# Attention scores of a graph network: source products made with folded query weights, biases by a row of ones

## What is computed

```python
q = x @ wq + bq
k = x @ wk + bk
v = x @ wv + bv
e = edge_attr @ we
ke = k[src] + e
score = jnp.sum(q[dst] * ke, axis=-1) / jnp.sqrt(jnp.asarray(ke.shape[-1], x.dtype))
smax = jax.ops.segment_max(score, dst, num_segments=n_nodes)
a = jnp.exp(score - smax[dst])
denom = jax.ops.segment_sum(a, dst, num_segments=n_nodes)
alpha = a / denom[dst]
msg = alpha[:, None] * (v[src] + e)
out = jax.ops.segment_sum(msg, dst, num_segments=n_nodes)
out = out + x @ ws + bs
```

## Time and profile before

| | us |
|---|---|
| median of 3 runs | 7116.05 (7091.61 to 7118.32) |
| profiled execution | 7111.88 |
| its span in the trace | 7110.1 |
| TensorE, VectorE, ScalarE, GpSimd busy | 4507.4, 4533.2, 1627.7, 4000.1 |
| last dense output of at1s, start | 3794.1 |
| last dense output of at2s, start | 5066.4 |

### The profile page before, as it was taken

How to read it: one execution, slowest core, us unless ns; L and a number is a source line. 1 busy time by engine, 2 the same in 40 slices (tenths; PEclk the granted TensorE clock), 3 DMA queues, 4 the chain that set the end, 5 groups by cost and what they waited for, 6 DMA issues and landing times. The chain is left out here.

```text
span 7110.1 us, 101720 instructions
## 1 busy us (share of the span) xinstructions
PE 4507.4 (63%) x31722; PEld 4047.3 (57%) x31722; DVE 4533.2 (64%) x5921; ACT 1627.7 (23%) x2291; POOL 4000.1 (56%) x3348
## 2 busy tenths in 40 slices
PE   4666335771067878266665846777587765784797
PEld 2355234661057778266665846666587764673675
DVE  6999544220567778399998833333687974782458
ACT  0044112330033344133332421111144430000001
POOL 0099466556067768777762877775000007757766
PEclk9866667995589999678887978999899987997999
DMA  6498666664932257333333844444377872222109
GB/s 245 151 275 266 157 145 139 139 138 66 360 101 72 74 174 257 88 98 98 98 94 114 263 144 123 132 135 128 103 243 267 311 283 62 53 57 88 14 12 289
DMA packets 850501, 1076.78 MB, mean 151 GB/s; under 512 B 589151, under 2 KB 601844, under 8 KB 848956
## 3 DMA queue, kind: packets, MB, share of 16 engines
q1 hardware_dynamic: 547292, 794.01, 34.7%
q0 software_dynamic: 144256, 90.12, 8.9%
q10 hardware_dynamic: 158560, 187.31, 7.9%
HBM read 608.19 MB, written 469.22 MB: 152 GB/s over the span
## 5 line engine op out<-in xcount | busy, mean ns | idle before, releaser
L857 POOL DMA_INDIRECT gc_msgs<-t,src_rows x784 | 756.3, 965 | 1142.6 <-POOLq L147 847.1
L911 POOL DMA_INDIRECT acc<-de_sums,de_put x392 | 609.2, 1554 | 416.3 <-DMA acc<-de_sums,de_put 268.9
L1953 PEld LDWEIGHTS gc_ring<-gc_msgs,gc_hot 128*128 128x128 f32 x4736 | 621.1, 208 | 313.3 <-issue 305.2
L1953 PE MATMUL gc_ring<-gc_msgs,gc_hot 128*128 x4736 | 647.5, 295 | 238.1 <-SPq L1912 236.9
L857 POOL DMA_INDIRECT edge_rows<-h,dst_rows x392 | 478.0, 1219 | 242.2 <-DMA h<-at1w_win 126.0
L857 POOL DMA_INDIRECT edge_rows<-x,dst_rows x392 | 505.5, 1290 | 167.7 <-issue 117.1
L1045 PE MATMUL de_ring<-de_win,de_pick 128*128 x2368 | 343.9, 306 | 267.1 <-DMA de_win<-t 267.1
L1045 PEld LDWEIGHTS de_ring<-de_win,de_pick 128*128 128x128 f32 x2368 | 323.4, 218 | 289.3 <-issue 284.4
L857 POOL DMA_INDIRECT at1s_ends<-x,src_rows x392 | 398.0, 1015 | 150.5 <-issue 121.1
L857 POOL DMA_INDIRECT re_rows<-x,src_rows x392 | 408.7, 1043 | 125.3 <-issue 125.0
L857 POOL DMA_INDIRECT at2s_ends<-h,src_rows x392 | 372.9, 951 | 174.4 <-issue 116.5
(11 more groups left out here) (479 smaller groups left out, 11362.9 us busy)
## 6 DMA issues: line engine op xcount, KB each, us to landing
rew_win<-x SPq DMA_DIRECT2D x74, 544.0 KB
at1w_win<-g SPq DMA_DIRECT2D x74, 544.0 KB
at2w_win<-g SPq DMA_DIRECT2D x74, 544.0 KB, 4.1
de_near<-same SPq DMA_DIRECT2D x74, 512.0 KB, 5.2
de_win<-t SPq DMA_DIRECT2D x74, 512.0 KB, 4.5
x<-rew_win SPq DMA_DIRECT2D x74, 512.0 KB
h<-at1w_win SPq DMA_DIRECT2D x74, 512.0 KB
h<-at2w_win SPq DMA_DIRECT2D x74, 512.0 KB, 2.9
```

The source lines that it names most:

```text
L857: nc.gpsimd.indirect_dma_start(buf[:, t * width:(t + 1) * width], None, table, bass.IndirectOffsetOnAxis(ap=rows[:, t:t + 1], axis=0)).the ...
L911: nc.gpsimd.indirect_dma_start(g.acc0[j % 2], bass.IndirectOffsetOnAxis(ap=put[:, j:j + 1], axis=0), sums[:, j * D:(j + 1) * D], None, com ...
L1953: done = nc.tensor.matmul(ring[:, bass.ds(to[n], SLOT)], hot[k][:, n, :], each_group(msgs[:, bass.ds(of[n], MID)], SLOT // MID), start=Fal ...
```

## The change

Scores are computed as relu(x_dst) . u, where u holds, for every edge, the query weights times (k + e): the weights wk·wqᵀ and [we; bk]·wqᵀ are made once per stage, on TensorE, by `lay_out` on VectorE and ten lines ahead of TensorE's batches. The query bias becomes one more column for each tile of a pair, so a product is 258 columns wide: 128 of u, 128 of v, 2 of bias terms. Four of these fill four banks, psU. Attributes are transposed into 64 rows (4 transposes in place of 2), and a 65th row of ones brings the biases of k and v. Destination rows are no longer scaled, transposed, copied with relu or multiplied: `dot` reads them where they lie, relu and product in one instruction, and the sum is scaled afterwards (8 columns) in at1s. ScalarE's new step `keep` copies v to the destination rows' place and the bias terms into `scores`; `score` then adds the two. The dense products of at2s come 256 columns wide, both weights side by side. ScalarE's order is written out.

The last pair comes four times. The transposes of destination rows and the query products are gone, 14 transposes ahead of the pieces are 12, and 16 products are 8 wide ones. The core of the diff:

```diff
                 def turn(b):
                     ...
-                    for k in range(B // 2):
-                        nc.tensor.transpose(psD[:, k * P:(k + 1) * P], values[:, b.number * W + k * P:b.number * W + (k + 1) * P], g.ident[:, :])
-                    transpose_pairs(nc, psE, ea[s % 2], g.ident, B // 4)
+                        nc.tensor.transpose(psE[0:D, k * P:(k + 1) * P], ea[s % 2][:, k * D:(k + 1) * D], g.ident[:, :])
                 def project(b):
                     ...
-                    times(nc, psQ, hdT[s % 2], wq, B // 2)
-                    for to, w in ((psK, wk), (psV, wv)):
-                        for h in range(2):
-                            nc.tensor.matmul(to[:, h * 256:(h + 1) * 256], eaT[s % 2][:, h * P:(h + 1) * P], we[:, :], start=True, stop=False,
-                                             skip_group_check=True)
...
+                    for j in range(B // 2):
+                        nc.tensor.matmul(psU[:, j, 0:PUT], eaT[s % 2][0:D + 1, j * P:(j + 1) * P], from_attr[:, :], start=True, stop=False,
+                                         skip_group_check=True)
+                        last = nc.tensor.matmul(psU[:, j, 0:PUT], hsT[s % 2][:, j * P:(j + 1) * P], from_src[:, :], start=False, stop=True,
+                                                skip_group_check=True)
 # own
-                            times(nc, psY, xT[s % 2][:, h * W:(h + 1) * W], g.w[dense[n][0]], B // 2).then_inc(piece, 1)
+                            times(nc, psY, xT[s % 2][:, m * EACH * P:(m + 1) * EACH * P], own_w, EACH).then_inc(piece, 1)
 # ScalarE
-                    nc.scalar.activation(hdT[s % 2][:, :], psD[:, :], ACT.Relu)
+                def keep(b):
+                    act.wait_ge(dotted, b.number + 1)
+                    nc.scalar.activation(grouped(far(b), P), psU[:, :, P:2 * P], ACT.Copy)
+                    nc.scalar.activation(grouped(scores[:, bass.ds(b.number * B, B)], 2), psU[:, :, 2 * P:PUT], ACT.Copy).then_inc(used, 1)
-                    pipeline(act, order=[(1, root), (1, turn), (0, square), (4, nothing)], slots=SLOTS)
+                    written_out(order=[(1, root), (2, keep), (1, turn), (0, square)], slots=SLOTS)
 # VectorE
-                    nc.vector.tensor_tensor(grouped(far(b), D), grouped(far(b), D), spread(root[:, 0, B:J], D), ALU.mult)
+                def dot(b):
+                    if not normalise:
+                        dve.wait_ge(ahead[b.slot], 16 * B * b.nth)
+                    dve.wait_ge(product, b.number + 1)
+                    nc.vector.scalar_tensor_tensor(grouped(dots[:, :], P), grouped(far(b), P), 0.0, psU[:, :, 0:P], ALU.max, ALU.mult).then_inc(dotted, 1)
+                    dve.wait_ge(dotted, b.number + 1)
+                    link(nc.vector.tensor_reduce(found[:, :], grouped(dots[:, :], D), AXX, ALU.add))
+                    if normalise:
+                        link(nc.vector.tensor_tensor(found[:, :], found[:, :], sd[b.slot % 2][:, 0, B:J], ALU.mult))
                 def score(b):
...
+                    at = scores[:, bass.ds(b.number * B, B)]
                     dve.wait_ge(used, b.number + 1)
+                    link(nc.vector.tensor_tensor(at, at, found[:, :], ALU.add))
                     link.restart()
...
+                    pipeline(dve, order=[(1, variance), (1, scale), (2, dot), (2, take(0)), (2, score), (0, centre), (2, take(1))], slots=SLOTS)
+                    pipeline(dve, order=[(2, dot), (2, take(0, 1)), (2, score), (2, take(2, 3))], slots=SLOTS)
```

More of the change, by code:

```diff
@@ L1455, in attention_scores @@
     bq, bk, bv = (g.w[n] for n in biases)
-    pieces = [(h, n) for n in range(len(dense)) for h in range(2)]
-    M = len(pieces)
+    N2 = len(dense)
+    EACH = 4 // N2
+    M = J // 2 // EACH
+    PUT = 2 * P + 2
     with Room(nc, g, name + "s") as r:
@@ L1461, in attention_scores @@
         ea = [r.sb(f"ea{k}", [P, B * DE]) for k in range(2)]
-        outs = [[r.sb(f"out{n}{k}", [P, C]) for k in range(2)] for n in range(len(dense))]
-        hsT, hdT, eaT, xT = ([r.sb(f"{n}{k}", [P, w]) for k in range(2)] for n, w in (("hsT", W), ("hdT", W), ("eaT", B * DE), ("xT", C)))
-        q, k_ = g.zeros[:, 0:W], g.zeros[:, W:2 * W]
+        outs = [r.sb(f"outs{k}", [P, N2 * C]) for k in range(2)]
+        hsT, eaT, xT = ([r.sb(f"{n}{k}", [P, w]) for k in range(2)] for n, w in (("hsT", W), ("eaT", W), ("xT", C)))
+        dots, found = g.zeros[:, 0:W], g.zeros[:, W:W + B]
+        from_src, from_attr = r.sb("from_src", [P, PUT]), r.sb("from_attr", [D + 1, PUT])
+        key_rows, query_bias = r.sb("key_rows", [D + 1, P]), r.sb("query_bias", [P, P])
+        own_w = g.w[dense[0][0]] if N2 == 1 else r.sb("own_w", [P, N2 * P])
+        own_b = r.sb("own_b", [P, N2, 2, D])
+        tipped_w = xT[0]
+        KEY, ATTR, QUERY, BIAS = 0, P, 2 * P, 3 * P
         if normalise:
@@ L1507, in inputs_ready @@
                 eng.wait_ge(got[b.slot], 16 * B * b.nth)
-                eng.wait_ge(ahead[b.slot], 16 * B * b.nth)
                 eng.wait_ge(ea_in[b.slot], 32 * b.nth)
@@ L1597, in _, with lay_out @@
                 link = Link(dve, link_s)
+                def lay_out():
+                    v = nc.vector
+                    v.tensor_copy(key_rows[0:D, :], we[0:D, 0:P])
+                    v.tensor_copy(grouped(key_rows[D:D + 1, :], D), each_group(bk[D:D + 1, :], 2))
+                    v.tensor_copy(grouped(query_bias[:, :], D), each_group(bq[:, :], 2)).then_inc(laid, 1)
+                    for k in range(2):
+                        v.memset(eaT[k][D:D + 1, :], 1.0)
+                    for n, (_, bias, _) in enumerate(dense):
+                        v.tensor_copy(own_b[:, n, :, :], each_group(g.w[bias][:, :], 2))
+                        if N2 > 1:
+                            v.tensor_copy(own_w[:, n * P:(n + 1) * P], g.w[dense[n][0]][:, :])
+                    v.tensor_copy(from_src[:, P:2 * P], wv[:, :])
+                    v.tensor_copy(from_attr[0:D, P:2 * P], we[0:D, 0:P])
+                    v.tensor_copy(grouped(from_attr[D:D + 1, P:2 * P], D), each_group(bv[D:D + 1, :], 2))
+                    link(v.memset(tipped_w[:, BIAS:BIAS + 2], 0.0))
+                    dve.wait_ge(tipped, 1)
+                    v.tensor_copy(tipped_w[:, 0:ATTR + D + 1], psS[:, 0:ATTR + D + 1])
+                    v.tensor_copy(tipped_w[:, QUERY:QUERY + P], psS[:, QUERY:QUERY + P])
+                    v.tensor_copy(tipped_w[0:D, BIAS:BIAS + 1], psS[0:D, BIAS:BIAS + 1])
+                    v.tensor_copy(tipped_w[D:P, BIAS + 1:BIAS + 2], psS[D:P, BIAS:BIAS + 1]).then_inc(folded, 1)
+                    dve.wait_ge(combined, 1)
+                    for to, ps in ((from_src[:, :], psX[:, :]), (from_attr[:, :], psY[0:D + 1, :])):
+                        v.tensor_copy(to[:, 0:P], ps[:, 0:P])
+                        last = v.tensor_copy(to[:, 2 * P:PUT], ps[:, P:P + 2])
+                    last.then_inc(weights_made, 1)
                 def centre(b):
```

51 lines of the change are left out of this document (25 added, 26 removed).

## The result

The changed kernel takes 6997.1 us, median of four runs (6991.8 to 7009.3), against 7117.1 for the kernel before beside it. The forecast was 7008, range 6962 to 7062. The profiled execution has a span of 6994.7 us where the one before had 7110.1. Both were cut at the same points of the timelines: the start of the first source gather of a stage and the start of its last take.

A forecast was written before the change was run, and what follows sets the result against it. Up to batch 37 GpSimd's gathers were taken as the bound (level with VectorE in at1s), behind it VectorE in at1s and the TensorE-VectorE loop in at2s; -28-78=-106 us, forecast 7008, range 6962 to 7062.

The forecast's parts named there:

- At1s, first 38 batches: At1s up to batch 37: GpSimd, at 16.0 us per batch, hides VectorE's saving; likely value 0.
- At1s, last eleven batches: At1s behind batch 37: VectorE alone is the bound and saves 2.1 us per batch, 23 us in all.
- Drain -4 to -5: At1s after the last batches: two scores, one scaling and shorter products save 4 to 5 us.
- The lengthening of gathers: At1s, first 38 batches: VectorE instructions with two SBUF inputs stretch two gathers per batch, 1.0 us; expected unchanged.
- an estimate in proportion: At1s, first 38 batches: two of seven large contenders go, 11 us more won; low end of less-stretch rival, chance 0.05.
- More than two per batch: Sign against the forecast: gathers of 1.44 us more often than twice per batch; more-stretch rival, +48 at most, chance 0.08.
- At2s: -78: At2s: 75.7 us won by batch 48, with eleven loops of 11.8 us behind batch 37, and 2 in the drain.
- The 1.7 us for the lower clock: At2s, batch 37, from its transposes to its products: 1.7 us added for TensorE's lower clock after a long wait.
- The 0.3 for the clock: At2s loop behind batch 37: 0.3 us added to the sum of 11.5 for TensorE's lower clock level, giving 11.8.
- Drain -2.5 (-2): At2s after batch 48: the drain was forecast to lose 2 us more.
- Hidden parts: Both stages: ScalarE's copies and, at the head, folding the weights lie in waits and cost 0; folding at worst 10.
- Slower through the clock: Rival, at2s: the lighter TensorE falls to its lower clock level, loop up to 19.6 us, 7290 us; chance 0.04.

The follow-up runs named there:

- the second profile: The changed kernel run and profiled once more, unedited, for the scatter of its stages: 7010.0 us in this one run.
- e3: The kernel before with the change in at1s alone, at2s as before: 7074.3 us, 0.9958 of before.
- e2: The changed kernel without the 19x8 destination gathers inside each of the two stages: 6772.0 us, 0.953 of the kernel before.
- e4: The kernel before with the change in at2s alone, at1s as before: 7017.5 us, 0.9871 of before.
- e8: The changed kernel with ScalarE's copy of v made three times in each batch: 6996.3 us, 0.982 of the kernel before.
- e1: The kernel before without the 19x8 destination gathers inside each of the two stages: 7097.2 us, 0.998 of before.
- e6: The changed kernel with the row means and roots of at1s in PSUM in place of SBUF: 6964.3 us, 0.978 of the kernel before.

## Why the prediction was right, step by step

- **At1s, first 38 batches: 0.** Batch 37 begins 612.4 us after the first gather, before 609.2; in the second profile 608.7, in e3 609.0. The zero holds, and e2 shows what it hides: in both stages, 225 us.
- **At1s, last eleven batches: 11x2.1=-23.** Measured 16.01 to 13.83, -24.0. **Drain -4 to -5:** 29.3 to 26.7 from batch 48's first instruction to the last take, -2.6: the term was put too high. The stage: -28 forecast; -23.5, -27.5 and -30.1 in three profiles.
- **The lengthening of gathers.** The zero was in part luck. Two of seven contenders went, and an estimate in proportion gave 11 us less; up to batch 37 the lengthening is 36.4 us before and 41.9, 38.1 and 38.5 with the change. The reason given for the zero, that the two scalings that stretch gathers both stay, does not hold: before, 77 of the stage's 95 lengthened gathers start inside those two; after, only 46 of 137 do, and the other 91 inside the three centrings. What counts is not how many such instructions there are but whether a gather starts inside one. VectorE meets them oftener, 108 lengthened gathers up to batch 37 in place of 75, presumably because it now starts a batch when a gather lands; no run tests that reason. More than two per batch was one of the signs that I named as speaking against the forecast. It came, but at 5.5 us at most: more gathers are hit, each for less.
- **At2s: -78, measured -84.2 and, in e4, -85.8.** The mechanism holds; its terms were mis-sized by a little. Batch 37's product came 580.3 us after the first gather, where 585.1 was forecast. Its last gather ends 4.0 us earlier: I had taken GpSimd's time from the kernel before, where 12 gathers of at2s are lengthened (2.5 us) by the product of q and k, which goes, and the other gathers took 0.947 us there and 0.944 here (1.4 us over 456 of them, an estimate). From there to the transposes 1.5 in place of 2.1, and to the product 9.77 (4802.71 to 4812.48) in place of 10.0. The 1.7 us for the lower clock measured 1.4: the loop above needs 4906.53-4898.20=8.33 from its transposes to the product. The transposes of that batch, after their wait, take nearly twice as long as those in that loop (0.60), and the 9.77 us are granted 0.85, where that loop has 1.00:

```profile
4802.71 1.12 PE L693 MATMUL at2s_psS<-ident,at2s_ends 128*128 128x128 f32 x4 [2.61 <-DMA at2s_ends<-h,src_rows]
```

  The loop is 11.68 on average ((708.8-580.3)/11) and 11.59 when steady, against 11.8. The 0.3 for the clock measured nothing, as all eleven are granted 1.00 (row above); what is over 11.59 is the first loop of 12.76, in which batch 38's transposes still wait for a gather:

```profile
4816.84 0.66 PE L693 MATMUL at2s_psS<-ident,at2s_ends 128*128 128x128 f32 x4 [0.94 <-DMA at2s_ends<-h,src_rows]
```

  Together this is 1.3 us over the eleven. Drain -2.5 (-2).
- **Hidden parts.** ScalarE's copies (e8) and the folding of weights (the first gather to the first product of at2s 22.3 us, before 23.2) cost nothing, as forecast. The cover of the folding is smaller than the 102 us that the forecast names: VectorE's part of it starts in at1s at 2968.85, with the stage, ends at 2974.57, and 6.15 us are left until the first source rows land.
- **Slower through the clock.** At2s was granted 0.89, under 0.91, but the loss lies up to batch 37, where TensorE waits for gathers anyway; behind it the clock rose from 0.93 to 1.00.
- Nothing of the forecast's sum depends on the 10 us of the lead-in; without them the profiles differ by 105, and the runs by 112 with 18 us either way. The two stages give -108 in the first profile and -111 in the second, against -106.

## What to carry to other kernels

A saving on one engine counts in full only in the stretch in which that engine sets the pace; find the instruction on the other queue at which the pace changes hands (here the last destination gather), and price the whole saving from there on. Ahead of it a saving counts only down to the other engine's pace: nothing in at1s, where both needed 16.0 us a batch, and 36 us in at2s, where it was 16.0 against 15.0. Then ask what the new bound's queue could do in another order: spreading the same gathers won some 50 us, a quarter of the 225 that they hid. To prove a hidden saving, take the cover away from both versions: e1 and e2 differ by 325 us where the kernels differ by 112.

## What was not expected of the hardware

- An indirect gather of 128 rows occupies GpSimd for 0.94 us, and up to 1.99 when it starts inside a VectorE instruction with two SBUF inputs; it then ends 0.81 to 0.83 us behind that instruction. With one of the two inputs in PSUM it never exceeds 0.953, and VectorE is no slower (0.69 for 128x512). In at1s this is worth 38 to 42 us (e6).
- Lengthened gathers differ from one execution to the next of the same code: 52.5 and 47.6 us in sum, and the stage with them, 791.2 and 787.1.
- The fused relu-and-multiply with one operand in PSUM takes 0.67 to 0.69 us for 128x512, as long as a plain product of that shape (0.68 to 0.69).
